# Routed layer: weights by tanh of the logits' difference between the Gelus, and tiny Gelus ahead of four tanh groups

## What is computed

```python
logits = _gelu(xf @ w_r1 + b_r1) @ w_r2 + b_r2          # 8 experts
top_p, top_i = jax.lax.top_k(jax.nn.softmax(logits), 2)
top_p = top_p / jnp.sum(top_p, axis=-1, keepdims=True)
for _ in range(2):
    ctx = concatenate([integrated, v])
    ctrl = _gelu(ctx @ w1 + b1) @ w2 + b2               # per expert, and for the shared one
    # alpha = sigmoid, beta = softplus, gate = sigmoid of the three parts of ctrl
    v_next = alpha * v - beta * (integrated - mu)
    x_next = integrated + 0.1 * gate * v_next           # summed over the experts with top_p
    halt = sigmoid(_gelu(x_next @ w_h1 + b_h1) @ w_h2 + b_h2)
    refined = _gelu(x_next @ w_f1 + b_f1) @ w_f2 + b_f2
    integrated = integrated + halt * refined * integration_weight
```

## Time and profile before

| | us |
|---|---|
| median of 3 runs | 810.71 (810.64 to 810.85) |
| the profiled execution's own time | 810.27 |
| its span in the profile | 808.5 |

### The profile page before, as it was taken

How to read it: one execution, slowest core, us unless ns; L and a number is a source line. 1 busy time by engine, 2 the same in 40 slices (tenths; PEclk the granted TensorE clock), 3 DMA queues, 4 the chain that set the end, 5 groups by cost and what they waited for, 6 DMA issues and landing times. The chain is left out here.

```text
span 808.5 us, 15028 instructions
## 1 busy us (share of the span) xinstructions
PE 718.2 (89%) x5042; PEld 401.9 (50%) x5042; DVE 550.9 (68%) x1749; ACT 497.0 (61%) x1343; POOL 170.3 (21%) x161
## 2 busy tenths in 40 slices
PE   5988996899998788999689999798989999779887
PEld 3666773566664322333256666453346666544222
DVE  8799978599984478487757999844066655436543
ACT  4788863588883667697658889326665655322101
POOL 7412300641102166256542000201000000000000
PEclk9999998799998869998879999889999999969999
DMA  5793000570000000000007100000000000000000
GB/s 204 149 306 146 2 2 1 109 181 6 2 2 1 0 0 1 1 0 1 0 5 156 19 2 2 27 1 0 0 1 2 1 1 1 1 1 0 2 0 26
DMA packets 17356, 27.59 MB, mean 34 GB/s; under 512 B 1408, under 2 KB 15360, under 8 KB 16640
## 3 DMA queue, kind: packets, MB, share of 16 engines
q1 hardware_dynamic: 17280, 26.64, 12.2%
HBM read 19.03 MB, written 7.60 MB: 33 GB/s over the span
## 5 line engine op out<-in xcount | busy, mean ns | idle before, releaser
L899 ACT ACTIVATE RING<-RING,NMX 128x256 f32<-128x256 f32 x384 | 190.9, 500 | 36.6 <-DVE NMX L1851 36.5
L1851 DVE CUSTOM_DVE_ANT_0 RING<-bank,ADJM 128x256 f32<-128x256 f32 x384 | 144.0, 414 | 19.2 <-PE bank L1270 12.7
L1317 PE MATMUL bank<-W,RING 128*128 128x128 f32 x768 | 117.3, 278 | 14.1 <-ACT RING L911 12.7
L1317 PEld LDWEIGHTS bank<-W,RING 128*128 128x128 f32 x768 | 88.1, 142 | 35.7 <-ACT RING L899 26.6
L1863 DVE COPY RING<-bank 128x512 f32<-128x512 f32 x144 | 98.6, 686 | 7.7 <-PE bank L1317 7.2
L559 POOL TENSOR_TENSOR small<-small 128x2 f32<-128x2 f32 (+2 forms) x16 | 19.0, 1188 | 347.8 <-DVE small L1723 347.8
L899 ACT ACTIVATION_READ_ACCUMULATOR RING<-RING,NMX 128x1 f32 x384 | 72.7, 189 | 0.0
L814 ACT ACTIVATE RING<-bank,NMX 128x512 f32<-128x512 f32 x64 | 43.4, 683 | 42.0 <-PE bank L1204 21.3
L1469 PE MATMUL bank<-ARENA,W 64*128 64x512 f32 x180 | 62.4, 709 | 3.5 <-DVE ARENA L2067 2.2
L1791 DVE TENSOR_REDUCE NMX<-bank 128x1 f32<-128x512 f32 x64 | 39.4, 678 | 31.9 <-PE bank L1171 31.9
L1335 PE MATMUL bank<-RING,ARENA 128*32 128x256 f32 x768 | 60.8, 390 | 0.2
(11 more groups left out here) (268 smaller groups left out, 1316.1 us busy)
## 6 DMA issues: line engine op xcount, KB each, us to landing
scratch<-ARENA SPq DMA_DIRECT2D x18, 192.0 KB, 2.7
ARENA<-scratch SPq DMA_DIRECT2D x6, 576.0 KB, 8.3
W<-in_weights SPq DMA_DIRECT2D x1, 2564.0 KB, 22.9
scratch<-ARENA SPq DMA_DIRECT2D x18, 128.0 KB, 2.8
ARENA<-scratch SPq DMA_DIRECT2D x6, 384.0 KB, 6.3
W<-in_weights SPq DMA_DIRECT2D x2, 1024.0 KB, 14.2
W<-in_weights SPq DMA_DIRECT2D x1, 1905.5 KB, 15.4
scratch<-ARENA SPq DMA_DIRECT2D x18, 64.0 KB, 7.9
```

Of the source, the lines that this page charges most:

```text
L899: nc.scalar.activation(P_OF(n)[:, q * S:(q + 1) * S], S_OF(n)[:, q, :], ACT.Exp, bias=NMX[:, 2 * t + q:2 * t + q + 1], scale=-1.0, accum_o ...
L1317: mm = nc.tensor.transpose(bk[:, o:o + P], P_OF(n)[:, i:i + P], ident)
L1851: nc.vector.tensor_tensor_reduce(out=S_OF(n)[:, q, :], in0=SBANK(n)[:, q * S:(q + 1) * S], in1=ADJM[:, b, q, :], scale=-1.0, scalar=BIG, o ...
```

## The change

The two weights come from Tanh instead of Exp: DVE makes FAR8, the logits minus half the second largest, inside `top2(1)`; ACT takes its Tanh after the third group of `hidden(1)` instead of an Exp after the fifth; DVE multiplies (Tanh + 1) by the selection, which has been scaled by a quarter of the routed share ahead of time. PE does the router one group of `hidden(0)` earlier, `weight_rows()` after two groups of `betas(0)` and ahead of the others, as transposes, and waits for the cast rows only in front of the first `weights`. DVE casts the rows before it multiplies the shared expert's beta. And at four places of ACT's order `gelu_tables()`, a Gelu of one column into `WARM`, stands between Softplus and Tanh groups.

```diff
+        FAR8 = RING[:, 12, 128:192].rearrange("p (t e) -> p t e", t=NT)
...
+            def gelu_tables():
+
+                nc.scalar.activation(WARM, col("mu"), ACT.Gelu)
+
             hidden(0, (0, 1, 2, 3, 4))
-            hidden(1, (0, 1, 2, 3, 4))
-            act.wait_ge(s_log, 1)
-            nc.scalar.activation(EXPL, LOG, ACT.Exp).then_inc(s_el, 1)
+            hidden(1, (0, 1, 2))
+            act.wait_ge(s_far, 1)
+            nc.scalar.activation(EXPL, FAR8, ACT.Tanh).then_inc(s_el, 1)
+            hidden(1, (3, 4))
...
             betas(1, (0, 1, 2, 3, 4, 5, 6, 7))
+            gelu_tables()
             gates(1, (0, 1, 2, 3))
             refine(0)
...
             betas(2, (NE, 0, 1))
+            gelu_tables()
             alphas(2, (0, 1))
             hidden(3, (0, 1, 2))
             alphas(2, (2, 3))
             betas(2, (2, 3, 4, 5))
+            gelu_tables()
             alphas(2, (4, 5))
             hidden(3, (3, 4))
...
             betas(3, (6, 7))
+            gelu_tables()
             alphas(3, (6, 7))
             refine(2)
...
                     for i in range(4):
-                        mm = nc.tensor.matmul(bk[0:3 * NE, i * P:(i + 1) * P], XN[:, 4 * c + i, 0:3 * NE], ident,
-                                              start=True, stop=True)
+                        mm = nc.tensor.transpose(bk[0:3 * NE, i * P:(i + 1) * P], XN[:, 4 * c + i, 0:3 * NE], ident)
                     mm.then_inc(s_fb, 1)
-                pe.wait_ge(s_eb, rb.n)
...
-            hidden(0, (0, 1, 2))
+            hidden(0, (0, 1))
             router()
-            hidden(0, (3, 4))
+            hidden(0, (2, 3, 4))
             hidden(1, (0, 1, 2, 3, 4))
-            betas(0, (NE, 0, 1, 2, 3))
+            betas(0, (NE, 0))
+            weight_rows()
+            betas(0, (1, 2, 3))
             gates(0, (NE,))
-            weight_rows()
+            pe.wait_ge(s_eb, rb.n)
             weights(0, (0, 1))
...
                 link(nc.vector.tensor_reduce(MX2[:, :, 0], REST8, AX.X, ALU.max))
+                if n == 1:
+                    nc.vector.scalar_tensor_tensor(FAR8, MX2.to_broadcast([P, NT, NE]), -0.5, LOG, ALU.mult,
+                                                   ALU.add).then_inc(s_far, 1)
...
             top2(1)
+            dve.wait_ge(s_el, 1)
+            link(nc.vector.tensor_scalar(SWI, SWC, -0.25, 0.25, ALU.mult, ALU.add))
+            chain(nc.vector.tensor_scalar(SWC, SWC, 0.5, 0.5, ALU.mult, ALU.add))
+            dve.wait_ge(s_sel, 1)
+            link(nc.vector.tensor_scalar(SEL, SEL, SWI, None, ALU.mult))
             dve.wait_ge(s_el, 2)
-            dve.wait_ge(s_sel, 1)
-
-            link(nc.vector.tensor_tensor(WT8, EXPL, SEL, ALU.mult))
-            chain(nc.vector.tensor_scalar(SWI, SWC, -0.5, 0.5, ALU.mult, ALU.add))
-            link(nc.vector.tensor_reduce(DEN, WT8, AX.X, ALU.add))
-            chain(nc.vector.tensor_scalar(SWC, SWC, 0.5, 0.5, ALU.mult, ALU.add))
-            link(nc.vector.reciprocal(RDEN, DEN))
-            link(nc.vector.tensor_scalar(RDEN, RDEN, SWI, None, ALU.mult))
-            link(nc.vector.tensor_tensor(WT8, WT8, RDEN3.to_broadcast([P, NT, NE]), ALU.mult))
+            link(nc.vector.scalar_tensor_tensor(WT8, EXPL, 1.0, SEL, ALU.add, ALU.mult))
...
             settle()
+            spread()
             first(0, (NE,))
             second(0, (NE,))
-            spread()
             first(0, (0, 1, 2, 3))
```

More of the change, by code:

```diff
@@ L361, in program @@
         s_log = sem("s_log")
+        s_far = sem("s_far")
         s_el = sem("s_el")
```

## The result

The changed kernel takes 804.61 us (median of 20 runs, 799.57 to 821.72) against 810.63 (20 runs, 806.20 to 818.35) of the kernel before. The ratio is 0.9928, 95% interval 0.9910 to 0.9946: faster by 0.7%, some 5.8 us. The forecast was 802.2. Runs of one kernel spread over some 10 us here, and a few that were disturbed on the chip are left out of all ratios.

The account below looks back on a forecast made before the run. Bounds, in the routed layer: a chain of small routing steps, ACT and DVE alternating, PE from 318 to 358, then ACT and DVE. Terms -5.0 - 0.5 + 0 - 1.0 - 2.0 + 0 = -8.5 from 810.71 gave 802.2 us, range 799.5 to 806.5.

Parts of the forecast that it names:

- signs of being wrong: first(0,0) not before 279, a load before a Tanh behind a tiny Gelu, or clock 0.50 in the PE-bound stretch.
- Head: Routed layer's start, routing through gates(2 to 5): earlier Tanh, parts and weight rows give -5.0 us, bounds -3.5 and -7.5.
- The new wait for first(0,0): In the head: first(0,0) queues on DVE behind second(NE); PE still idles some 2 us at 276 to 278.
- the half that I had added for the clock: In the head: clock back before betas(4,5) and the following weights, half a microsecond more beyond 4.4 us.
- First tiny Gelu: Before refine(0): the load at 309.99 goes, wf2 matmuls move from 313.24 to 312.7; -0.5 us, bounds 0 and -1.1.
- Second and fourth: Before hidden(3,(0,1,2)) and refine(2): saved loads hidden by PE and DVE, 0 each; second -1.1 uncovered, fourth at worst +0.2.
- Third: Before hidden(3,(3,4)): load at 356.32 goes, ACT reaches the gates 1.09 earlier; -1.0 us, bounds -0.2 and -1.6.
- The clock behind it: After the third tiny Gelu: PE keeps 2.4 GHz over the former 0.51 stretch; -2.0 us, bounds 0 and -2.5.
- Sum: All terms of the routed layer: -5.0 - 0.5 + 0 - 1.0 - 2.0 + 0 = -8.5 us.
- the rival of the loads that stay: At the four tiny Gelus: Gelu loads stay, each costs up to 0.19 on ACT; 806.2 us, chance 3%.
- The rival with a low clock in the PE-bound stretch: From 318 to 358: shifted layer brings 1.2 GHz there, making the kernel slower; fifteen microseconds give 817; chance 3%.

Follow-up runs that it names:

- e3: Changed kernel with only the third tiny Gelu (first, second and fourth calls removed); ratio to the kernel before 0.9877 (0.9815 to 0.9939).
- e10: Changed kernel with weight_rows() moved back behind betas(0,(1,2,3)) and gates(0,NE); ratio to the kernel before 0.9908 (0.9873 to 0.9943).
- e12: Changed kernel without the third tiny Gelu, keeping the other three; ratio to the kernel before 0.9927 (0.9897 to 0.9957).
- e1: Changed kernel without its four tiny Gelus, the routing part alone; ratio to the kernel before 0.9908 (0.9875 to 0.9941).
- e5: The kernel before, run and profiled again with no edit; ratio to the kernel before 1.0020 (0.9997 to 1.0042).
- e6: The changed kernel, run and profiled again with no edit; ratio to the kernel before 0.9910 (0.9873 to 0.9947).
- e7: Changed kernel with its weight rows as 16 plain matmul instructions instead of 8 transposes; ratio to the kernel before 1.0007 (0.9973 to 1.0042).
- e9: Changed kernel with the logits' Tanh after the fifth Gelu of hidden(1) instead of the third; ratio to the kernel before 0.9983 (0.9957 to 1.0009).

## Why the prediction was right, and where not

The time lies in the stated range and the sign is right; the gain was put at 8.5 us, and measured at 5.8, 6.95 in the layer itself. The range was wide enough for four of its terms to come out short together. None of the signs of being wrong came: counted from the start of the layer first(0,0) starts at 26.01 (27.7 was the limit), no load stands between a tiny Gelu and the Tanh behind it, and the clock is 1.00 from 318 to 358. By its own steps:

- **Head, -5.0: measured -4.63.** The small steps came as worked out. Counted from the start of the layer, against the profile before: parts ready 4.4 earlier (expected 4.3); rows 3.8 earlier (4.0); gates(2 to 5) 283.86 instead of 283.30 with a start 4.76 later, so 4.2 earlier (4.4); first spread weights 5.9 earlier (5.2), because cutting the beta groups cost 0.27 (1.98 + 1.99 against 3.70) and not 0.86. The new wait for first(0,0) was named in advance. Behind gates(2 to 5) another 0.4 came, about the half that I had added for the clock. But the clock did not do what I had said: it was back before betas(4,5) and then fell again from 34.2 to 41.1. The low time of the head went from 20.5 to 10.3 us, and that it came out near my half microsecond is luck, since the same head code reached refine(0) at 51.5 to 54.7 as the low stretches fell.
- **First tiny Gelu, -0.5: measured 0.** The wf2 matmuls do come 0.3 earlier (313.06 with the later start). But DVE's integrate(0), before and after,

```profile
316.02 0.94 DVE L2117 SCALAR_TENSOR_TENSOR ARENA<-ARENA 128x512 f32<-128x512 f32 x1 [1.83 <-ACT ARENA L992]
```

```profile
315.87 1.24 DVE L2128 SCALAR_TENSOR_TENSOR ARENA<-ARENA 128x512 f32<-128x512 f32 x1 [1.53 <-ACT ARENA L994]
```

takes 0.3 longer when it starts earlier, and ends at the same place. In both it ends 0.55 us behind the end of one of POOL's adds in SBUF (316.41 and 316.56); that DVE waited for this add is argued from these rows, not tested. This step of the prediction failed: I took the path from PE's matmuls to hidden(2) as fixed in length.
- **Second and fourth, 0: measured 0** (e3 against e10). As worked out.
- **Third, -1.0: measured -0.76** (e3 against e12). The idle before 363.80 fell only from 1.13 to 0.91, since DVE's chain in front of it moved by hardly more than PE's.
- **The clock behind it, -2.0: measured -1.6.** The low stretch went from 7 us to 3, not to none. At full clock it would have been -2.2. The sum's number is nearly right, its reason is not shown: I had the clock stay up because PE's idle before two of its groups goes. In e12 and e1 the third tiny Gelu is missing, in e12 the idle of 1.13 is back, and the clock is full; the changed kernel has 0.91 of idle like e3's 0.90, and its clock falls where e3's does not. So this term agrees by luck, and what places the low stretch stays open.
- **Sum.** -4.63 - 0.76 - 1.6 make the layer's 6.95, to rounding. The difference to 5.8 lies outside. In the repeated profiles, e5 and e6, it adds up: -6.87 in the layer, +0.45 in front of it and +0.4 behind it are the -6.0 between their 810.10 and 804.10 us. No line changed in front or behind; the stages behind took 401.8 us in the kernel before and 400.8 to 405.6 in the others.
- **Small errors of the text ahead.** The Tanh of 0.26 does not fit into ACT's gap of 0.17 before its next Gelu, but that Gelu still started 0.86 behind the one before, at 272.56. And -5.0 with four times 0.19 gives 806.5 for the rival of the loads that stay, not 806.2.

Where the prediction failed is thus one term, the first Gelu, and the clock: I priced the clock as part of two steps, while it hits all that stands behind. e7 shows the size: 0.9 us of work became 4.1 in the layer and the whole gain in the time. The rival with a low clock in the PE-bound stretch did not come. In the changed kernel no load stands between the tiny Gelu (L999), the four tanh groups of the gates and refine's Gelu, and the 27 loads became 22: the Exp's and one for each of the four tiny Gelus. A load in front of a tanh group was thus decided by the function that stood there first, not by the Gelus that follow it; the Trainium skill ("ScalarE activation tables: per-element evaluation and per-set limits", section "Table sets in the compiler and the runtime") has the compiler place loads for the longest run that one set serves, and the trace disagrees. PE's clock stayed at 1.00 for 7 us behind the eight transposes; so no run shows an effect of what the Trainium skill says ("TensorE: Matmul & The Clock Gate", section "Part 4: PE-mode transpose"), that transposes do not count as activity for the clock.

Open: how often the low stretch of the first attention comes to each kernel, and what of 5.8 us is luck in where the later stages start. No run takes apart the Exp's saved load, the DVE steps that went with it, and the casts ahead of first(NE).

## What to carry to other kernels

Load saving counts only where ACT is late: of five saved table loads, one stood in the chain that all waited for (the Exp's; no run prices it alone) and one gave 0.76 us; three gave nothing. Look for the small chain that everything waits for, and shorten it at its slowest step: taking the Tanh between the Gelus, and transposes for matmuls, carried this gain, for without either of them (e9, e7) the time was no longer clear of the kernel before. Measure a change of less than 1% with marks inside the changed stage, from more than one profile, because a shift of a microsecond can move the clock's low stretches over all that follows.

## What the runs showed of the hardware

- A transpose of 128x24 in single precision into PSUM is one instruction; eight took 1.05 us where sixteen plain matmul instructions took 1.93, both at full clock (e7). At half clock the eight took 1.88 (e9).
- The same code from the start of the layer to refine(0) took 51.51, 51.53, 52.88, 52.95 and 54.74 us, with the granted clock as the difference that the profiles show (over 27 to 45 us 0.81 in e3 and e12, 0.72 in after, e6 and e1; e1 has half clock from 48 to 55 us too).
- PE was busy without a break from 279.4 to 290.0 in the kernel before, and its clock stayed at 0.50 all that time.
- Two executions of one kernel agreed within 0.1 us over 155 us of a layer, low stretches and all.
